# Splitting the next layer's projection weights in sixteen parts inside the layer before it

## The chip, the cores and the metric

One core of one Trainium2 chip runs the whole program. The metric is the device time of one execution in microseconds (us). The kernel before took 4826.84 us (median of three runs, 4824.58 to 4827.53). Lower is better.

## The reference, cut to what matters

Four blocks over 16 sequences of 256 tokens and 128 features, each followed by a layer norm of x plus the block's output. The third is a gated scan, the fourth six layers of local attention with a feed-forward part; the first two (causal attention, a routed feed-forward) are not touched.

```python
    # third block: g, v, d are x times Wg, Wv, Wd plus biases
    x_scan = sigmoid(g) * tanh(v);  a = 0.001 + 0.998 * sigmoid(d)
    h_t = a_t * h_(t-1) + x_scan_t
    # fourth block, per layer i of 6: 16 heads of 64, windows of 32 and the window before
    for i in range(DEPTH):
        x = attn_layer(shift_tokens(x), Wqkv[i], q_scale[i], k_scale[i], Wo[i]) + x
        x = ffn_layer(shift_tokens(x), ln_g[i], ln_b[i], W1[i], b1[i], W2[i], b2[i]) + x
    # attn_layer: qkv = x @ Wqkv (128 x 3072); q and k to unit length, scaled, rotated; softmax in windows; @ Wo
x = _layernorm(x + scan(x)); x = _layernorm(x + six_layers(x))
```

## The kernel before, in words

The stream of tokens stays in SBUF, features on the partitions: `X` is 128 x 16 sequences x 290 columns (34 of padding). Blocks of code follow each other; between two blocks all engines meet at a barrier, and GpSimd clears the block's semaphores one by one (`clear_semaphores`, line 30).

**The gated scan** (`gated_scan`) works a sequence at a time. VectorE scales the normed result into `X0` (line 1758), GpSimd copies it from there into `X` (line 1726). `X0` stays in SBUF through the six layers, since the last norm (`add_and_norm` with tag "o") adds it to the layers' output (line 1518), half a thousand columns at a time, eight times.

**The six layers** (`local_attention_layers`) are 192 tiles of 128 tokens: 6 layers x 16 sequences x 2. Each engine runs its own program of slots; in slot k it works on tile k and on tiles up to seven behind, `tile(n)` being the tile n behind. The functions in `slot` stand in each engine's order. Even slots belong to the first half of a sequence, odd ones to the second; a turn of a loop is one even and one odd slot. TensorE has one flat loop over all sequences (`run_flat`, 92 turns in the middle, so 184 tiles of the 192), in which the layer of tile k is `k >> 5`; the other engines have a loop over layers with four sequences of each layer written out and the rest in an inner loop.

- `product` (TensorE, line 2055) multiplies a tile by a chunk of 512 columns of the layer's weights; there are six chunks, q1, k0, q0, k1, v0, v1. For precision both sides are split in a high part (upper bits) and a low part (the rest), and a product is three matmuls, high x high, high x low, low x high. Each product waits for its chunk's split (line 2052). Within a slot TensorE does q1 and k0, down, centred, q0 and k1, then v1 of the tile before, variance, project, the turns of queries and keys, hidden_up, the turns of attention and probabilities, hidden_gate, scores (128 small matmuls, line 2141), v0, attend (128 small matmuls, line 2174).
- `split_weights` (VectorE, lines 2554 to 2558) makes the two parts of a chunk: a mask by bits into `W_cut`, a copy to `W_high`, a subtraction to `W_low`. Five chunks are split in the first slot of a layer, after the normalised attention and ahead of the tables (line 2540) and the first rotation (line 2572); v1 is split one slot later, since the last tile of the layer before still reads it.
- `load_projections` (SP, line 1974) loads a layer's whole weights (1536 KB) into `W_whole` in one DMA, two slots after the layer's start, for the next layer, and the scales of q and k (line 1975).
- `spread` (SP, lines 1992 to 1996) copies a tile's values into windows, six DMAs in an even slot and eight in an odd one. SP also loads the small weights of each layer one by one as the tile before stops using them (lines 2011 to 2035); while it waits for that, the spreads behind stand.
- GpSimd adds the sine parts (line 2489), multiplies queries and keys by their inverse lengths (line 2499, needs VectorE's line 2593), and splits and shifts the input (lines 2451 to 2476).
- VectorE's slot ends the tile before's key rotation and goes on: squared lengths (2582), gated (2656), denominators (2617, 2619), row maxima (2600, needs the scores), inverse lengths (2589, 2593), centred scores (2609), normalised attention (2627), rotations (2572), and the write of X for the tile seven behind (2664).

## Time and profile before

| what | us |
|---|---|
| median of three runs | 4826.84 |
| the profiled execution | 4830.08 |
| its span, first to last instruction | 4828.3 |
| TensorE busy | 4226.8 |
| VectorE busy | 3910.9 |
| ScalarE busy | 3408.1 |
| GpSimd busy | 2756.9 |

Durations come from the one profiled execution; between its span and its own time lie 1.8 us outside the first and last instruction. In the rows PE is TensorE's matmuls, PEld its weight loads, DVE VectorE, ACT ScalarE, POOL GpSimd and SP SyncE; L12 is line 12. A name with q behind it (PEldq, POOLq, SPq) is the engine's sequencer: register steps, branches, semaphores, the issue of DMAs. Busy time is a union, so that a matmul that overlaps the next counts once.

### The profile page before, as it was taken

Reading aid. Unit: us, or ns where it says so; the run is one execution under the profiler, and the core shown is the slowest. Engines: PE = TensorE matmul, PEld = TensorE weight load, DVE = VectorE, ACT = ScalarE, POOL = GpSimd, SP = SyncE. Lnnn points to the kernel's source line nnn. Section 1 sums busy time; section 2 is a strip of 40 time slices with the busy share of each in tenths; the row PEclk is TensorE's granted clock in tenths of the full one; section 3 lists DMA queues with packets and bytes.
Section 4 is the critical chain, followed back from the end, with each engine's and each line's share of the span. In section 5 each row is a group of like instructions: output and inputs, shape, how many; then the busy total and the mean of one; then the engine's idle time right before and its main releaser. Section 6 shows DMA issues by size and latency. Waiting matters only on the chain. (4 is left out here: it accounts for less than half of the span.)

```text
span 4828.3 us, 192699 instructions
## 1 busy us (share of the span) xinstructions
PE 4226.8 (88%) x74096; PEld 3380.5 (70%) x74097; DVE 3910.9 (81%) x6558; ACT 3408.1 (71%) x5995; POOL 2756.9 (57%) x3213
## 2 busy tenths in 40 slices
PE   7888875697455799999999999989999999999996
PEld 4444432375233688888888888878887888888884
DVE  5777757644446889999999999999999999989995
ACT  4555521254225689888998889879998898889983
POOL 2222213634221767767776777767776777677771
PEclk8999977798777999999999999999999999999997
DMA  3000003252210211111111211121112111121110
GB/s 149 1 0 0 0 0 117 92 197 75 98 57 18 65 38 48 47 55 53 43 47 49 59 48 41 48 59 47 48 42 60 49 46 46 40 69 41 48 45 28
DMA packets 141882, 255.16 MB, mean 53 GB/s; under 512 B 34160, under 2 KB 56944, under 8 KB 137072
## 3 DMA queue, kind: packets, MB, share of 16 engines
q1 hardware_dynamic: 133520, 235.49, 16.5%
q0 software_dynamic: 8192, 17.84, 1.2%
q8 instruction: 53, 0.87, 0.1%
q14 instruction: 117, 0.96, 0.1%
HBM read 70.76 MB, written 44.04 MB: 24 GB/s over the span
## 5 line engine op out<-in xcount | busy, mean ns | idle before, releaser
L2489 POOL TENSOR_TENSOR d_rc<-d_rc,d_rs 128x512 f32<-128x512 f32 x768 | 964.1, 1277 | 479.1 <-DVE d_rs L2572 463.3
L2499 POOL TENSOR_TENSOR d_rc<-d_rc,d_inv 128x1024 f32<-128x1024 f32 x384 | 722.9, 1903 | 123.3 <-DVE d_inv L2593 122.9
L2055 PE MATMUL d_pair<-d_W_high,d_xs_high 128*128 128x512 f32 x1152 | 520.7, 452 | 124.0 <-DVE d_W_low L2558 40.7
L2572 DVE TENSOR_TENSOR d_rc<-d_pair,d_rot 128x512 f32<-128x512 f32 x768 | 527.3, 687 | 97.2 <-ACT d_sq L2304 78.9
L2304 ACT ACTIVATE d_sq<-d_pair 128x512 f32<-128x512 f32 x768 | 435.3, 596 | 144.2 <-PE d_pair L2055 139.0
L2572 DVE TENSOR_TENSOR d_rs<-d_pair,d_rot 128x512 f32<-128x512 f32 x768 | 521.7, 679 | 0.0
L2055 PE MATMUL d_pair<-d_W_high,d_xs_low 128*128 128x512 f32 x1152 | 462.8, 402 | 0.0
L2055 PE MATMUL d_pair<-d_W_low,d_xs_high 128*128 128x512 f32 x1152 | 462.1, 401 | 0.0
L2582 DVE TENSOR_REDUCE d_ss<-d_sq 128x16 f32<-128x1024 f32 x384 | 448.0, 1207 | 0.0
L2202 PE MATMUL d_pair<-d_OT,d_Wo 128*128 128x128 f32 x3072 | 382.8, 279 | 0.0
L2055 PEld LDWEIGHTS d_pair<-d_W_high,d_xs_high 128*128 128x128 f32 x1152 | 220.2, 191 | 212.1 <-issue 153.7
L2099 PE MATMUL d_pair<-d_ident,d_rc 128*128 128x128 f32 x3072 | 367.7, 273 | 1.0 <-ACT d_sq L2304 1.0
L2202 PEld LDWEIGHTS d_pair<-d_OT,d_Wo 128*128 128x128 f32 x3072 | 367.1, 196 | 0.1
L2099 PEld LDWEIGHTS d_pair<-d_ident,d_rc 128*128 128x128 f32 x3072 | 342.8, 142 | 2.1 <-issue 1.7
L2600 DVE TENSOR_REDUCE d_mx<-d_pair 128x16 f32<-128x1024 f32 x192 | 234.5, 1221 | 104.5 <-PE d_pair L2141 104.5
L2141 PEld LDWEIGHTS d_pair<-d_KT,d_QT 64*32 64x32 f32 x24576 | 255.8, 105 | 89.6 <-issue 89.2
L2320 ACT ACTIVATE d_QT<-d_pair 128x1024 f32<-128x1024 f32 x192 | 196.8, 1025 | 158.9 <-PE d_pair L2099 158.9
L2174 PEld LDWEIGHTS d_pair<-d_VW,d_PT 64*32 64x32 f32 x18432 | 253.5, 105 | 76.2 <-issue 76.1
L315 ACT ACTIVATE a_first<-a_bank,a_late_bias,a_later 128x256 bf16<-128x256 f32 x256 | 130.1, 569 | 236.2 <-PE a_bank L163 236.2
L2174 PE MATMUL d_pair<-d_V,d_PT 64*32 64x64 f32 x6144 | 288.1, 227 | 7.1 <-issue 7.1
L2141 PE MATMUL d_pair<-d_KT,d_QT 64*32 64x64 f32 x24576 | 287.9, 225 | 7.3 <-issue 7.3
L2174 PE MATMUL d_pair<-d_VW,d_PT 64*32 64x64 f32 x18432 | 286.6, 227 | 6.5 <-issue 6.5
(370 smaller groups left out, 11236.5 us busy)
## 6 DMA issues: line engine op xcount, KB each, us to landing
d_VW<-d_V SPq DMA_DIRECT2D x768, 128.0 KB
d_VW<-d_V SPq DMA_DIRECT2D x576, 64.0 KB
leaf_rows<-a_zeros SPq DMA_DIRECT2D x12, 1152.0 KB, 14.8
q_xrow<-leaf_rows SPq DMA_DIRECT2D x24, 576.0 KB
leaf_out<-q_yrow SPq DMA_DIRECT2D x24, 512.0 KB
d_W_whole<-Wqkv_dram SPq DMA_DIRECT2D x7, 1536.0 KB, 6.2
f_xrow<-leaf_rows SPq DMA_DIRECT2D x8, 576.0 KB, 3.8
b_table<-q_w_dram SPq DMA_DIRECT2D x4, 1024.0 KB, 9.4
```

The costliest lines, as they stand in the source:

```text
L2055: mm = nc.tensor.matmul(target, x_part[:, t.par, :], w_part[:, c, :], start=n == 0, stop=n == 2)
L2099: mm = nc.tensor.transpose(ps[:, hp // 4, (hp % 4) * 128:(hp % 4) * 128 + 128], source(hp), ident[:])
L2141: mm = nc.tensor.matmul(s_pair[WIN * w:WIN * w + WIN, odd, hp * DH:hp * DH + DH], QT[rows, hp, WIN * w:WIN * w + WIN], KT[rows, hp, at + W ...
L2174: mm = nc.tensor.matmul(o_pair[WIN * w:WIN * w + WIN, odd, hp * DH:hp * DH + DH], PT[rows, hp, WIN * w:WIN * w + WIN], window_values(t, w, ...
L2202: mm = nc.tensor.matmul(proj_bank[:, 0:128], Wo[:, hp, :], OT[:, hp, :], start=hp == 0, stop=hp == HP - 1)
L2304: nc.scalar.activation(sq[:, half, 512 * j:512 * j + 512], ps[:, j, :], ACT.Square).then_inc(s[f"s{qk}{j}_ready"], 1)
L2320: nc.scalar.activation(QT[:].rearrange("p h t -> p (h t)"), flat_pair(qt_pair), ACT.Copy).then_inc(s["qt_ready"], 1)
L2489: nc.gpsimd.tensor_tensor(own[:, :, a, :], own[:, :, a, :], other[:, :, 1 - a, :], ALU.add).then_inc(s[f"add{qk}_ready"], 1)
L2499: nc.gpsimd.tensor_tensor(heads(rc[:, t.par, half, :]), heads(rc[:, t.par, half, :]), inv[:, t.par, half, :].unsqueeze(2).to_broadcast([12 ...
L2572: ins = nc.vector.tensor_tensor(heads(target), heads(ps[:, j, :]), rot[:, t.par, half, cs, :].unsqueeze(1).to_broadcast([128, HP, DH]), AL ...
L2582: nc.vector.tensor_reduce(ss[:, half, :], heads(sq[:, half, :]), AX_X, ALU.add).then_inc(s[f"ss{qk}_ready"], 1)
L2600: nc.vector.tensor_reduce(mx[:], s_pair[:].rearrange("p a (h n) -> p (a h) n", n=DH), AX_X, ALU.max)\
```

## The change

The weights have a second home: `W_high` and `W_low` are twice as long, and a layer's parts stand in the half of its parity. During layer l the weights of layer l + 1 are split in 16 parts of 192 columns, one in each even slot: SP loads the part into `W_stage` (96 KB, two places in turn), VectorE masks it into `W_next`, GpSimd subtracts and copies into the other half. TensorE waits for parts at q1 and v1 only, and reads the weights at a place worked out from the layer's parity. The first layer's weights are loaded whole into `W_first`, which lies in the space of `rc`, and split ahead as before, all six chunks. To make room, the scan's result `X0` is written to DRAM a sequence at a time and read back by the last norm. The part of layer 6 that nobody uses is split as well (96 parts in all, 16 a layer).

```diff
-def add_and_norm(nc, dram, X, Y, tag, leaf=None, out=None, s_out=None):
+def add_and_norm(nc, dram, X, Y, tag, leaf=None, kept=None, out=None, s_out=None):
+        names += [f"y_in{b}" for b in range(NB)]
@@ SP
+            if kept is not None:
+                for b in range(NB):
+                    sp.dma_start(Y[:, BT * b:BT * b + BT], kept[:, BT * b:BT * b + BT]).then_inc(s[f"y_in{b}"], 16)
@@ VectorE, summed(b)
+                if kept is not None:
+                    dve.wait_ge(s[f"y_in{b}"], 16)
@@ gated_scan, SP
+            for k in range(SEQS):
+                sp.wait_ge(s["x_ready"], k + 1)
+                sp.dma_start(kept[:, T * k:T * k + T], X0[:, T * k:T * k + T]).then_inc(s["stored"], 16)
+            sp.wait_ge(s["stored"], 16 * SEQS)
@@ local_attention_layers
-        W_high = sb("d_W_high", [128, W_CHUNKS, 512], F32R)
-        W_low = sb("d_W_low", [128, W_CHUNKS, 512], F32R)
-        W_whole = sb("d_W_whole", [128, W_CHUNKS, 512])
+        W_high = sb("d_W_high", [128, 2 * W_CHUNKS, 512], F32R)
+        W_low = sb("d_W_low", [128, 2 * W_CHUNKS, 512], F32R)
+        W_stage = sb("d_W_stage", [128, 2 * W_PART])
+        W_next = sb("d_W_next", [128, 2 * W_PART])
+        def next_part(w, t):
+            half = (t.l + 1) % 2 if isinstance(t.l, int) else (t.l + 1) & 1
+            return w[:].rearrange("p c n -> p (c n)")[:, bass.ds(half * (W_CHUNKS * 512) + t.b * W_PART, W_PART)]
@@ SP
+            def load_next_part(t):
+                if not t.live or t.par:
+                    return
+                n = t.l * W_PARTS + t.b
+                sp.wait_ge(s["next_split"], n + 1)
+                sp.sem_inc(s["gate_sp"], 1)
+                whole = of_layer("Wqkv", t.l + 1).rearrange("o p c n -> p (o c n)")
+                sp.dma_start(W_stage[:, turn_of(n)], whole[:, bass.ds(t.b * W_PART, W_PART)]).then_inc(s[f"w_in"], 16)
...
                 spread(tile(2))
                 t = tile(2)
                 if t.live and t.first:
-                    sp.wait_ge(s["w_split"], W_CHUNKS * t.l + W_CHUNKS)
-                    sp.sem_inc(s["gate_sp"], 1)
                     sp.wait_ge(s["tables"], 8 * t.l + 8)
                     sp.sem_inc(s["gate_sp"], 1)
-                    load_projections(t.l + 1)
+                    load_scales(t.l + 1)
+                load_next_part(tile(0))
@@ TensorE
+            def weights(w_part, t, c):
+                if t.edge:
+                    return w_part[:, t.l % 2 * W_CHUNKS + c, :]
+                return w_part[:, bass.ds((t.l & 1) * W_CHUNKS + c, 1), :].rearrange("p o n -> p (o n)")
             def product(t, target, what):
                 c = CHUNK_OF[what]
-                if t.first:
-                    pe.wait_ge(s["w_split"], W_CHUNKS * t.l + c + 1)
+                if t.edge:
+                    if t.first:
+                        pe.wait_ge(s["w_split"], c + 1)
+                elif what == "q1":
+                    pe.wait_ge(s["next_split"], t.l * W_PARTS)
+                elif what == "v1":
+                    pe.wait_ge(s["next_split"], t.l * W_PARTS + 2)
                 wait(pe, "xs_split", t)
                 for n, (x_part, w_part) in enumerate(((xs_high, W_high), (xs_high, W_low), (xs_low, W_high))):
-                    mm = nc.tensor.matmul(target, x_part[:, t.par, :], w_part[:, c, :], start=n == 0, stop=n == 2)
+                    mm = nc.tensor.matmul(target, x_part[:, t.par, :], weights(w_part, t, c), start=n == 0, stop=n == 2)
@@ GpSimd, after add_sine_part(tile(2), 0, "q"): next_weights(tile(4)); ahead of all: pool.sem_inc(s["next_split"], 2)
+            def next_weights(t):
+                if not t.live or t.par:
+                    return
+                n = t.l * W_PARTS + t.b
+                pool.wait_ge(s["next_cut"], n + 1)
+                pool.sem_inc(s["gate_pool"], 1)
+                cut = W_next[:, turn_of(n)]
+                nc.gpsimd.tensor_tensor(next_part(W_low, t), W_stage[:, turn_of(n)], cut, ALU.subtract).then_inc(s["next_low"], 1)
+                nc.gpsimd.tensor_copy(next_part(W_high, t), cut).then_inc(s["next_split"], 1)
@@ VectorE; split_weights is left for the first layer alone, mask, subtraction, copy, all six chunks in slot 0
+            def next_cut(t):
+                if not t.live or t.par:
+                    return
+                n = t.l * W_PARTS + t.b
+                dve.wait_ge(s["w_in"], n * 16 + 32)
+                dve.wait_ge(s["next_split"], n + 1)
+                dve.sem_inc(s["gate_dve"], 1)
+                nc.vector.tensor_scalar(W_next[:, turn_of(n)].bitcast(U32), W_stage[:, turn_of(n)].bitcast(U32), 0xFFFFF000, None,
+                                        ALU.bitwise_and).then_inc(s["next_cut"], 1)
...
-                split_weights(tile(1), ("v1",))
                 denominators(tile(3))
+                next_cut(tile(0))
                 row_maxima(tile(2))
                 inverse_lengths(tile(1))
                 centred_scores(tile(2))
                 normalised_attention(tile(3))
-                split_weights(tile(0), ("q1", "k0", "q0", "k1", "v0"))
+                split_weights(tile(0), ("q1", "k0", "q0", "k1", "v0", "v1"))
                 tables(tile(0))
```

## Rows read from the trace of the kernel before

**Rows 1.** The page: busy tenths of TensorE in 40 slices of the span.
```profile
PE   7888875697455799999999999989999999999996
```

**Rows 2.** Windows, one turn (even and odd tile): busy us of PE, PEld, DVE, ACT, POOL; clock; DMA.
```profile
2428.50:2460.30 31.80, 31.35 (x695) 27.81 (x694) 29.92 (x50) 28.74 (x52) 23.74 (x29) 1.00 0.17 45
```

**Rows 3.** Waits in 2240 to 2580, TensorE's only one: us in total, times, longest.
```profile
PE d_pair L2055 <- issue: 4.3, 10, 0.5
```

**Rows 4.** Timeline of VectorE: start, us, instruction; X written for tiles 22, 28 and 32.
```profile
2044.55 0.34 DVE L2664 SCALAR_TENSOR_TENSOR X<-d_pair,d_vecs_a,XM 128x128 f32 x1
...
2151.28 0.34 DVE L2664 SCALAR_TENSOR_TENSOR X<-d_pair,d_vecs_a,XM 128x128 f32<-128x128 f32 x1
...
2219.08 0.34 DVE L2664 SCALAR_TENSOR_TENSOR X<-d_pair,d_vecs_a,XM 128x128 f32<-128x128 f32 x1
```

**Rows 5.** Timelines of VectorE, GpSimd, TensorE at the split; all masks by line (ns min/median/max).
```profile
2090.58 2.08 DVE L2554 TENSOR_SCALAR d_W_cut<-d_W_whole 128x512 uint32<-128x512 uint32 x1
...
2100.01 1.16 DVE L2540 TENSOR_TENSOR d_rot<-d_rot_const,d_qkscale 128x64 f32<-128x64 f32 x8
...
2088.62 3.76 POOL L2499 TENSOR_TENSOR d_rc<-d_rc,d_inv 128x1024 f32<-128x1024 f32 x2 [0.85 <-DVE d_inv L2593]
...
2093.86 0.79 PE L2055 MATMUL d_pair<-d_W_high,d_xs_high 128*128 128x512 f32 x1 [4.83 <-DVE d_W_low L2558]
...
L2554 DVE TENSOR_SCALAR d_W_cut<-d_W_whole x36: 410/427/2079, 1562.1 to 4212.0; 128x512 uint32<-128x512 uint32 x36
```

**Rows 6.** Timelines of SP and VectorE: last DMA of an even spread, steady and late.
```profile
2447.61 0.60 SPq L1996 DMA_DIRECT2D d_VW<-d_V  x1
...
2196.34 0.60 SPq L1996 DMA_DIRECT2D d_VW<-d_V  x1
...
2197.75 1.23 DVE L2600 TENSOR_REDUCE d_mx<-d_pair 128x16 f32<-128x1024 f32 x1 [1.93 <-PE d_pair L2141]
```

**Rows 7.** Timelines of an even slot: VectorE, GpSimd's input split, TensorE's v1 product.
```profile
2451.26 0.25 DVE L2619 RECIPROCAL d_rden<-d_den 128x16 f32<-128x16 f32 x1
2451.86 1.23 DVE L2600 TENSOR_REDUCE d_mx<-d_pair 128x16 f32<-128x1024 f32 x1 [0.35 <-PE d_pair L2141]
...
2456.22 0.69 DVE L2572 TENSOR_TENSOR d_rc<-d_pair,d_rot 128x512 f32<-128x512 f32 x1 [0.46 <-ACT d_sq L2304]
...
2451.61 0.46 POOL L2476 TENSOR_TENSOR d_xs_low<-d_xs,d_xs_high 128x128 fp32r<-128x128 f32 x1
...
2458.32 0.40 PE L2055 MATMUL d_pair<-d_W_high,d_xs_high 128*128 128x512 f32 x1
```

**Rows 8.** Timelines of VectorE and GpSimd at the end of the scan.
```profile
1550.29 0.42 DVE L1758 TENSOR_TENSOR X<-c_xc,c_rstd 128x256 f32<-128x256 f32 x1
...
1550.92 0.40 POOL L1726 COPY X<-X 128x256 f32<-128x256 f32 x1 [4.24 <-DVE X L1758]
```

**Rows 9.** DMA issues: count, KB each, median us to landing.
```profile
out_dram<-X SPq DMA_DIRECT2D x8, 256.0 KB, 2.1
```

**Rows 10.** Register steps by line (ns min/median/max); on TensorE's timeline, an even slot's q1 product.
```profile
L2052 PEldq ALU_OP  x828: 32/32/32, 1697.2 to 4711.3; - x166
...
L1674 PEldq FUSED_REGOPS  x14: 55/62/69, 1456.5 to 1534.9; - x14
...
L963 PEldq ALU_OP  x448: 32/36/41, 936.0 to 1362.5; - x150
...
L963 PEldq FUSED_REGOPS  x256: 55/55/70, 936.1 to 1362.6; - x128
...
L1942 PEldq COMPARE_BRANCH  x92: 76/208/223, 1739.5 to 4713.7; - x92
...
2454.54 0.49 PE L2055 MATMUL d_pair<-d_W_high,d_xs_high 128*128 128x512 f32 x1 [0.41 <-issue]
```

**Rows 11.** GpSimd's first operation in the last norm, and all clears of semaphores.
```profile
4777.74 0.10 POOL L1494 MEMSET o_eps<- 128x1 f32 x1 [19.02 <-POOLq L26]
...
L30 POOLq EVENT_SEMAPHORE_RANGE_CLEAR  x271: 37/44/48, 713.1 to 4827.9; - x136
```

More of the change, by code:

```diff
@@ L1640, in gated_scan @@
         names = """w_in memset_done gates_done gate_ready u_ready a_ready h_ready r_ready mean_done xc_ready
[L1641 removed]
+            xsq_ready var_done std_ready rstd_ready x_ready copied gate stored""".split()
         s = {n: ctx.enter_context(nc.semaphore("c_" + n)) for n in names}
@@ L1782 @@
 W_CHUNKS = len(CHUNK_OF)
+W_PARTS = 16
+W_PART = W_CHUNKS * 512 // W_PARTS
 SPREADS = (6, 8)
@@ L2521, in slot @@
                 add_sine_part(tile(2), 0, "q")
+                next_weights(tile(4))
                 shifted_input(tile(1))
@@ L2544, in split_weights @@
             def split_weights(t, whats):
-                if not (t.live and t.first):
+                if not (t.live and t.first and isinstance(t.l, int)):
                     return
-                dve.wait_ge(s["w_in"], 16 * t.l + 16)
+                dve.wait_ge(s["w_in"], 16)
                 for what in whats:
                     c = CHUNK_OF[what]
-                    wait(dve, f"{what}_done", t, -1)
-                    if c or not isinstance(t.l, int):
-                        dve.wait_ge(s["w_split"], W_CHUNKS * t.l + c)
-                    nc.vector.tensor_scalar(W_cut[:].bitcast(U32), W_whole[:, c, :].bitcast(U32), 0xFFFFF000, None, ALU.bitwise_and)\
+                    if c:
+                        dve.wait_ge(s["w_split"], c)
+                    nc.vector.tensor_scalar(W_cut[:].bitcast(U32), W_first[:, c, :].bitcast(U32), 0xFFFFF000, None, ALU.bitwise_and)\
                         .then_inc(s["w_cut"], 1)
-                    dve.wait_ge(s["w_cut"], W_CHUNKS * t.l + c + 1)
-                    nc.vector.tensor_copy(W_high[:, c, :], W_cut[:]).then_inc(s["w_high"], 1)
-                    nc.vector.tensor_tensor(W_low[:, c, :], W_whole[:, c, :], W_cut[:], ALU.subtract).then_inc(s["w_split"], 1)
+                    dve.wait_ge(s["w_cut"], c + 1)
+                    nc.vector.tensor_tensor(W_low[:, c, :], W_first[:, c, :], W_cut[:], ALU.subtract).then_inc(s["w_low"], 1)
+                    dve.wait_ge(s["w_low"], c + 1)
+                    nc.vector.tensor_copy(W_high[:, c, :], W_cut[:]).then_inc(s["w_split"], 1)
+                dve.wait_ge(s["w_split"], W_CHUNKS)
+            def next_cut(t):
[7 more added lines that the diff above has]
+                                        ALU.bitwise_and).then_inc(s["next_cut"], 1)
             def rotated(t, half, qk, j):
@@ L2759, in build @@
         fast_feedforward_block(nc, dram, X, rows_dram, out_dram, scattered, gathered, arrived, bias_dram)
-        X0 = ctx.enter_context(nc.sbuf_tensor("X0", [128, SEQS * T], F32))
-        gated_scan(nc, dram, X, X0)
+        kept = nc.dram_tensor("scan_out", (128, SEQS * T), F32).ap()
+        with ExitStack() as inner:
+            X0 = inner.enter_context(nc.sbuf_tensor("X0", [128, SEQS * T], F32))
+            gated_scan(nc, dram, X, X0, kept)
         with ExitStack() as inner:
@@ L2764, in build @@
             local_attention_layers(nc, dram, X, XM)
-        add_and_norm(nc, dram, X, X0, "o", out=out, s_out=s_out)
+        X0 = ctx.enter_context(nc.sbuf_tensor("X0_again", [128, SEQS * T], F32))
+        add_and_norm(nc, dram, X, X0, "o", kept=kept, out=out, s_out=s_out)
 def kernel(**inputs):
```

19 lines of the change are left out of this document (11 added, 8 removed).

## The prediction

> **What bounds the kernel now.** I read the page first: span 4828.3 us, and from slice 15 on TensorE is at 9 tenths in nearly every slice [rows 1], so two thirds of the span is the six layers. Next came the windows of one even and one odd tile (two tiles are one turn of the loop): 31.80 us with TensorE busy 31.35, VectorE 29.92, ScalarE 28.74, GpSimd 23.74, at clock 1.00 [rows 2]. The waits of a steady stretch say who yields: VectorE and ScalarE wait for TensorE, GpSimd for VectorE, and TensorE waits for nobody; its idle time is "issue", 10 times 0.43 us in 10.7 turns [rows 3]. So in a layer TensorE sets the pace of 15.88 us a tile, and VectorE has 1.9 us to spare in a turn (31.80 - 29.92). Last, the timeline of VectorE's X writes (one a tile): from tile 22's to tile 28's 106.73 us pass where six steady tiles take 95.3, and from there to tile 32's 67.80 for 63.5 [rows 4]. A change of layer loses 11.4 us around the weight split and, four tiles later, 4.3 us. My readings of the other four changes are 12.9, 13.0, 11.4, 12.7 and 4.3, 4.1, 4.1, 5.2, in all 61.4 and 22.0 us.
>
> The first loss is the split: VectorE spends 2090.58 to 2100.01 on five chunks (9.43 us; the first mask takes 2.08 us, the median one 427 ns), and TensorE stands 4.83 us before the first product of the layer [rows 5]. The second loss is another matter: SP is held by the small weights' waits, the last DMA of the spread starts at 2196.34, 1.4 us before VectorE's row maxima of that slot, where in steady state it starts 4.25 us before them [rows 6, 7].
>
> **Part 1, the split leaves the boundary.** The 15 instructions of the block go, the three of v1 one tile later too. What stays is the eight table products, 1.16 us [rows 5]. They delay the first rotation, and VectorE's idle before it (0.46) takes a part; the v1 product needs that rotation and has 0.8 us of margin (2458.32 against 2456.22 and two of 0.69, which overlap a little: 2457.5) [rows 7]. I leave 1.0 us a boundary, 5 in all: gain 61.4 - 5 = **56**. Bounds: 50 (2.3 stays each) to 61.
>
> **Part 2, VectorE's mask in every even tile.** 96 masks of 192 columns. 512 columns take 427 ns [rows 5], so 192 take between 160 (by columns alone) and 427, and I take 260 for a fixed part. It stands after the denominators' reciprocal, which ends at 2451.51, and before the row maxima, which wait for TensorE until 2451.86 [rows 7]. 0.35 us of idle cover 0.26; the register steps of its waits lie under the instruction before. If the cover goes, 0.46 us of idle before the rotation catch it. Cost 0. Above: GpSimd. The first mask of the layer ended at 2092.66, 0.28 us after GpSimd's pair of products (2088.62 + 3.76 = 2092.38) [rows 5]: such a mask does not run beside a GpSimd instruction. At 2451.51 GpSimd is at its input splits of 0.46 us, and its 1.9 us products cannot be there, since they wait for inverse lengths that VectorE makes only later in the slot [rows 7]. So at most 0.26 + 0.46 = 0.72, against 0.81 of idle in the slot: 0 again. The Trainium skill has this as a rule (SBUF — State Buffer, "SBUF: two separate sides"): the pair of ports is an exclusive lock, whoever starts first keeps it for the whole instruction. By that rule the sum is the same unless the longer GpSimd products are met, which rival C prices.
>
> **Part 3, GpSimd.** Subtraction and copy of 192 columns each: two inputs of 128 columns take 0.46 and of 1024 columns 1.88 (half of 3.76), the copy of 256 takes 0.40, so 0.56 + 0.35 and some 0.2 around them, 1.1 us a turn [rows 5, 7, 8]. GpSimd has 8 us a turn to spare [rows 2]. It delays the next slot's input split by up to 1.1; the even slot's is ready at 2451.61 + 0.46 = 2452.07 and its first product starts at 2454.54 [rows 7, 10], so there are some 2.5 us of cover and nobody waits. Cost 0; below 0 nothing, as work is only added; above, 0.3 us in each of 96 turns, if its products of the next slot start that much later and somebody waits, = 29.
>
> **Part 4, SP and the parts' arrival.** One more DMA behind the even spread's six, whose last issue ends at 2448.21 [rows 6]. A wait that is long satisfied, register steps and issue put the DMA at about 2448.6. It carries 96 KB; 256 KB land 2.1 us after issue [rows 9], so it lands at about 2450.7, 0.8 us before the mask asks. Cost 0 in steady state. In the slot with the late spread it does not fit: issue after 2196.94, landing near 2199.4, where VectorE's row maxima began at 2197.75 [rows 6]. VectorE comes 1.6 to 2 us late, 0.46 at least is caught by idle before the rotation, and TensorE's margin of 0.8 takes most of the rest: 0.5 a boundary, **2.5** in all (0 to 10). The next spread is 11 us away, and the burst of 1536 KB at each change of layer goes, which nobody waited for.
>
> **Part 5, TensorE's sequencer.** This is the price that decides. In the loop the weights now stand at a place worked out from the layer's parity: for each product two addresses, and of the six waits on the split two remain. The waits cost 828 small register steps in 92 turns, 9 a turn [rows 10]. Of address work there are two kinds of rows: three products sharing one simple address cost 14 steps in 14 slots, one each; an address with shift and mask (the table products) costs (448 + 256)/256 = 2.75 steps, and those are hidden under long matmuls, the matmuls that follow them show next to no idle. Inside a product (0.7 us of matmuls) I cost them at nothing, the matmuls cover them. But right behind the 128 small matmuls of "attend" nothing covers: the loop's branch adds 208 ns and two register steps there, and the even q1 product that follows shows 0.41 us idle, where the odd one shows none (one idle spot a turn) [rows 3, 10]. One step there costs about 0.12 us. How many are new? The wait is swapped one for one; an address is at least one step, at most 2.75, and some may be shared with the slot before. I take 1.25, 0.15 us a tile, 184 loop tiles: **+28**. Bounds: -9 (a saved wait at v0, behind the scores, and shared addresses) and 0.4 x 184 = +74.
>
> **Part 6, the ends.** The scan's block now ends with the last store: ready at 1550.71, plus 2.1 us for such a store, against 1551.32 for the end of GpSimd's copy [rows 8, 9]: **+1.5**. The last norm starts when the first 256 KB are back, 2.1 us and some 0.2 of issue after 4777.74, and the chain of the norm follows from its first sum [rows 9, 11]: **+2.3** (2 to 5). 21 more semaphores are cleared, 44 ns busy each [rows 11] and 0.067 with what lies between: **+1.4**. The first layer splits six chunks ahead instead of five, in three steps that no longer overlap, and saves the late v1: 0 (-1 to +3).
>
> **Sum.** -56 + 0 + 0 + 2.5 + 28 + 1.5 + 2.3 + 1.4 = -20.3. The profiled execution took 4830.1 (span 4828.3 and 1.8 around it), so 4809.8; the median of the three runs shown is 3.2 lower, 4826.84, so **4806**.
>
> **Rivals.** A, the sequencer hides it all: then -48.3, 4778.5 (with the saved wait 4770). For it: the table products' steps were hidden. Against: they stood behind long matmuls. B, the other side: the addresses are worked out afresh at q1. Without this part the change is worth 48.3 us, so it ends slower once 0.26 us a tile, some two steps, are exposed there; at 0.4 us it is 4826.8 - 48.3 + 74 = 4852. For it: 2.75 steps is the row nearest in form, with two addresses a product. Against: repeated expressions are shared in the scan's row. C, VectorE's mask meets a long GpSimd product or a part lands late in every turn: 1.9 + 0.26 - 0.81 = 1.35 us x 96 = 130, 4936; a part 1 us late gives (1.26 - 0.81) x 96 = 43, 4849. Against: the order of the slot. D, the change doesn't remove the loss at the boundary, since GpSimd's last parts or the tables hold TensorE: with half the gain left 4834. By the order of the slots the last part is split more than half a slot before the v1 product that needs it, so this has little for it.
>
> **How the numbers follow.** My forecast (4790 to 4822) has 0.50, A (below 4790) 0.17, B 0.20, C 0.09, D 0.04. A measurement of this kernel tells 0.2% (9.7 us) from no change. Below 4817.2 lie A and most of the forecast: 0.66. Within 4817.2 to 4836.5 lie the forecast's upper edge, half of B and D: 0.19. Above: 0.15. The range leaves out the deep end of A, and of B and C what is above 4838: 4776 to 4838.
>
> **What would show it.** Right: X writes 15.9 us apart through the change of layer but for 1 us, the 4.83 us idle gone, the clock 1.00 all through; the mask near 0.26 to 0.7 us in VectorE's idle before the maxima; two idle spots of TensorE at q1, near 0.55 in even and 0.15 in odd slots, a turn of 32.1 us instead of 31.8. Wrong: a turn still at 31.8 (A), or above 32.3 (B), masks of 1 to 2 us or waits on the stage's DMA in steady turns (C), a gap before the first product of a layer (D).

## The result, and the profile after

The changed kernel takes 4840.28 us (median of 20 runs, 4829.81 to 4850.72) where the kernel before takes 4824.19 on the same chip (20 runs): ratio 1.0034, 95% interval 1.0027 to 1.0041, 16 us slower. I had forecast 4806, 20 us faster; the time lies above the end of my range. The two profiled executions (4830.1 and 4833.4) stand only 3.3 us apart. The memset of c_eps, the start of the scan, ahead of which only eight more semaphores are cleared, comes 13 us earlier in the one of after (1431.6 against 1444.7), so I compare stages: the scan takes 112.1 us (108.4 before), the layers 3234.0 (3224.7), the last norm 54.0 (50.5), together 16.4 us more.

Of the page, the row that answers [rows 1], and the windows of one turn (columns as in [rows 2]):

```profile
span 4831.6 us, 196107 instructions
...
PE   7888875697445899999999999999999999999996
```
```profile
2418.29:2434.62 16.33, 15.82 (x347) 14.06 (x348) 15.23 (x25) 14.38 (x26) 12.88 (x17) 1.00 0.18 48
2434.62:2450.47 15.85, 15.47 (x346) 13.66 (x346) 15.16 (x26) 14.29 (x26) 11.55 (x15) 1.00 0.18 48
sum 32.18, PE 31.29 PEld 27.73 DVE 30.38 ACT 28.67 POOL 24.43; mean PE 15.65 PEld 13.86 DVE 15.19 ACT 14.34 POOL 12.22
```

The turn is 32.18 us, not 31.80. TensorE is busy as long as before (31.29 against 31.35); what grew is its idle time. Next come the largest wait of TensorE in the same steady stretch as [rows 3] (besides it there is one of 0.8 us for GpSimd's split of the input), and TensorE's timeline at an even and an odd q1 product:

```profile
PE d_pair L2097 <- issue: 9.1, 21, 0.7
```
```profile
2450.75 0.49 PE L2097 MATMUL d_pair<-d_W_high,d_xs_high 128*128 x1 [0.66 <-issue]
...
2466.63 0.49 PE L2097 MATMUL d_pair<-d_W_high,d_xs_high 128*128 x1 [0.23 <-issue]
```

Idle "issue" went from 4.3 to 9.1 us, and it now stands ahead of each q1, not of every second. The line of the products' matmuls, which had no register steps before, has the ones below. The 828 of [rows 10] belonged to the waits on the split; in their place stand 184, one a tile.

```profile
L2097 PEldq ALU_OP  x1380: 32/32/36, 1694.0 to 4715.4; - x198
...
L2097 PEldq FUSED_REGOPS  x1104: 55/60/69, 1694.1 to 4715.3; - x184
```

Two of them stand between the branch and the even q1 product at 2450.75 (the same line, from 2450.5 to 2450.75), where before there was none of this line:

```profile
L2097 PEldq ALU_OP  x1: 36/36/36, 2450.5 to 2450.5; - x1
L2097 PEldq FUSED_REGOPS  x1: 60/60/60, 2450.6 to 2450.6; - x1
```

The change of layer is read from X's writes for tiles 22, 28 and 32, as in [rows 4]:

```profile
2041.42 0.34 DVE L2732 SCALAR_TENSOR_TENSOR X<-d_pair,d_vecs_a,XM 128x128 f32 x1
...
2141.84 0.34 DVE L2732 SCALAR_TENSOR_TENSOR X<-d_pair,d_vecs_a,XM 128x128 f32<-128x128 f32 x1
...
2212.10 0.34 DVE L2732 SCALAR_TENSOR_TENSOR X<-d_pair,d_vecs_a,XM 128x128 f32<-128x128 f32 x1
```

Six tiles take 100.42 us (before 106.73), the four behind them 70.26 (before 67.80). So the split did leave the boundary, but less came of it than I had booked, and the second loss grew. At the start of the layer VectorE and GpSimd show this (compare [rows 5]):

```profile
2084.03 0.26 DVE L2625 TENSOR_SCALAR d_W_next<-d_W_stage 128x192 uint32<-128x192 uint32 x1 [0.46 <-issue]
...
2088.03 2.84 DVE L2596 TENSOR_TENSOR d_rot<-d_rot_const,d_qkscale 128x64 f32<-128x64 f32 x8
2091.22 0.69 DVE L2640 TENSOR_TENSOR d_rc<-d_pair,d_rot 128x512 f32<-128x512 f32 x1 [0.36 <-DVE d_rot L2596]
```
```profile
2086.07 3.77 POOL L2541 TENSOR_TENSOR d_rc<-d_rc,d_inv 128x1024 f32<-128x1024 f32 x2 [0.98 <-DVE d_inv L2661]
```
```profile
PE d_pair L2097 <- DVE d_rs L2640: 2.1, 1, 2.1
```

The eight table products take 2.84 us in place of 1.16: the first of them lasts until GpSimd's second long product ends (2086.07 + 3.77 = 2089.84). TensorE stands 2.1 us here and 3.0 to 3.2 us at the other four changes, for the rotation behind them. All runs are laid side by side here, from their traces: the layers' stage (memset of d_eps to that of o_eps), the steady turn, and the means over the five changes of layer of the six tiles and of the four behind them, all in us.

| run | ratio to before, 95% | layers | turn | six | four |
|---|---|---|---|---|---|
| before | 1 | 3224.7 | 31.77 | 107.6 | 67.9 |
| after (the change) | 1.0034 [1.0027, 1.0041] | 3234.0 | 32.17 | 102.2 | 70.2 |
| before_address | 0.9999 [0.9990, 1.0008] | 3222.4 | 31.77 | 107.8 | 68.2 |
| before_parity | 1.0088 [1.0071, 1.0104] | 3261.0 | 32.22 | 109.7 | 68.5 |
| before_kept | 1.0007 [0.9998, 1.0016] | 3219.8 | 31.76 | 108.0 | 68.4 |
| static_address | 0.9951 [0.9936, 0.9966] | 3189.7 | 31.72 | 100.7 | 69.2 |
| after_no_parts | 0.9932 [0.9916, 0.9948] | 3176.1 | 31.71 | 98.8 | 68.5 |
| after_tables_first | 1.0001 [0.9991, 1.0011] | 3214.4 | 32.17 | 98.6 | 70.1 |
| after_load_first | 1.0045 [1.0028, 1.0061] | 3235.1 | 32.17 | 102.4 | 70.0 |
| after_part3_early | 1.0027 [1.0016, 1.0037] | 3231.2 | 32.17 | 102.3 | 69.4 |
| after_by_layers | 1.0000 [0.9991, 1.0010] | 3217.5 | 31.73 | 104.7 | 69.9 |
| after_by_layers_tables_first | 0.9971 [0.9961, 0.9982] | 3202.6 | 31.74 | 102.0 | 69.9 |
| after_v0_last | 0.9895 [0.9880, 0.9909] | 3158.1 | 31.09 | 100.7 | 69.9 |
| before_v0_last | 0.9853 [0.9840, 0.9866] | 3152.6 | 30.75 | 106.4 | 66.9 |
| before_v0_last_again | 0.9855 [0.9842, 0.9867] | 3158.2 | 30.74 | 106.4 | 67.2 |
| after_by_layers_tables_first_v0_last | 0.9915 [0.9902, 0.9929] | 3175.3 | 31.00 | 103.3 | 69.7 |
| after_tables_part3_v0 | 0.9841 [0.9828, 0.9853] | 3141.0 | 31.09 | 96.8 | 69.3 |
| after_tables_part3_v0_again | 0.9856 [0.9841, 0.9871] | 3138.3 | 31.09 | 96.8 | 69.1 |
| after_tables_part3_v0_no_mask | 0.9827 [0.9813, 0.9840] | 3132.5 | 31.09 | 96.3 | 68.2 |
| after_tables_part3_v0_split_on_gpsimd | 0.9979 [0.9969, 0.9988] | 3209.1 | 32.09 | 98.3 | 68.8 |

The runs lie on several chips. On two of them the kernel before takes 5031 us in place of 4822 to 4824; the 200 us lie ahead of the layers (d_eps at 1755 us in before_address, 1553 in before), the layers' stage and the turn are the same. Ratios are to the kernel before on the same chip.

### The profile page after: what moved, and what is told of

Same layout as the page of the kernel before. It is cut to its first block and busy times, and to the rows that moved or that the text cites. A ratio compares the mean times of both kernels' runs of the same rounds, so it can differ in the third digit from the quotient of the medians.

```text
span 4831.6 us, 196107 instructions
## 1 busy us (share of the span) xinstructions
PE 4205.7 (87%) x74096; PEld 3366.4 (70%) x74097; DVE 3914.5 (81%) x6564; ACT 3409.5 (71%) x5995; POOL 2827.3 (59%) x3405
## 5 line engine op out<-in xcount | busy, mean ns | idle before, releaser
L2097 PE MATMUL d_pair<-d_W_high,d_xs_high 128*128 (+1 forms) x1152 | 518.3, 450 | 146.9 <-issue 75.4
L2097 PE MATMUL d_pair<-d_W_high,d_xs_low 128*128 (+1 forms) x1152 | 461.0, 400 | 0.0
L2097 PE MATMUL d_pair<-d_W_low,d_xs_high 128*128 (+1 forms) x1152 | 459.7, 399 | 0.0
```

The costliest lines, as they stand in the source:

```text
L2097: mm = nc.tensor.matmul(target, x_part[:, t.par, :], weights(w_part, t, c), start=n == 0, stop=n == 2)
```

## The experiments

### Is the longer turn TensorE's address work?

static_address fixes the weights' place in TensorE's code:

```diff
-                return w_part[:, bass.ds((t.l & 1) * W_CHUNKS + c, 1), :].rearrange("p o n -> p (o n)")
+                return w_part[:, c, :]
```

> This is the changed kernel, but TensorE always reads the first home of the weights, at a fixed address, and GpSimd writes all parts into the second (so layers 2 to 6 compute with the first layer's weights; the work and its shapes are the same). Theory S, two register steps exposed ahead of every q1 product cost 0.20 us a tile: the turn falls from 32.18 us back to 31.8, TensorE's idle time at q1 from 0.64 and 0.25 us (even, odd) to 0.42 and 0, and the time by 37 us, from 4840 to 4803 (ratio to the kernel before 0.9957). Rival V, the longer turn comes from the work added in each turn (VectorE's mask, GpSimd's two instructions, the DMA), not from TensorE's addresses: the turn stays at 32.2 and the time at 4840 (ratio 1.003).

before_address and before_parity put the address work into the kernel before, which has neither mask nor parts in its turn:

```diff
+                return w_part[:, bass.ds((t.l & 8) + c, 1), :].rearrange("p o n -> p (o n)")      (before_address)
+                return w_part[:, c, bass.ds((t.l & 1) * 8, 512)]                                   (before_parity)
```

> This is the kernel before, with one thing alone of the change: in the loop TensorE works out the weights' address of each product from the layer's number (a bit of it that is always zero, so the same weights are read). Theory S: the turn rises from 31.77 to 32.1 or 32.2 us, idle at q1 from 0.41 and 0 to some 0.64 and 0.25, and the time by about 37 us, to 4861 (ratio 1.0077). Rival V: a turn of 31.8 us and 4824 (ratio 1.000).

> This is the kernel before, with TensorE's address worked out in the loop from the layer's parity, as the change has it, but only 8 columns apart (each chunk has 520 columns in place of 512; odd layers read their weights 8 columns further, so they compute with shifted weights; the work is the same). before_address did not do this: its trace has the same register steps as before, the bit was known to be zero, so that run was a second copy of the kernel before (0.9999). Theory S: each product gains a step or two, two of them stand exposed ahead of q1; the turn rises from 31.77 to 32.1 to 32.2 us, idle at q1 from 0.41 and 0 to 0.64 and 0.25 us, ratio 1.0075. Rival V: turn 31.8, ratio 1.000.

Measured: without the address work the turn falls to 31.72 us, with it alone the kernel before rises to 32.22. The waits of static_address (340 us of steady stretch) and of before_parity (as long), and before_parity's steps:

```profile
PE d_pair L2096 <- issue: 4.1, 10, 0.4
```
```profile
PE d_pair L2060 <- issue: 8.7, 21, 0.7
```
```profile
L2060 PEldq ALU_OP  x1380: 32/32/36, 1694.0 to 4747.3; - x198
...
L2060 PEldq FUSED_REGOPS  x1104: 46/46/60, 1694.1 to 4747.2; - x184
```

The counts of steps on the product's line are those of the change, and so are the idle spots: 21 again, one a tile. Theory S holds, from both sides. The address work is worth 0.40 us a turn between the kernels before and after (32.17 - 31.77), 0.45 in before_parity and 0.45 in static_address: 0.20 to 0.23 us a tile. before_address changed nothing, since the bit was known to be zero and no step was made (its sequencer's counts are those of before): it is a second copy of the kernel before, whose 0.9999 shows what a null looks like.

### What do the parts cost?

after_no_parts is static_address without the load, the mask and GpSimd's two instructions.

```diff
-                nc.vector.tensor_scalar(W_next[:, turn_of(n)].bitcast(U32), W_stage[:, turn_of(n)].bitcast(U32), 0xFFFFF000, None,
-                                        ALU.bitwise_and).then_inc(s["next_cut"], 1)
...
-                nc.gpsimd.tensor_tensor(next_part(W_low, t), W_stage[:, turn_of(n)], cut, ALU.subtract).then_inc(s["next_low"], 1)
-                nc.gpsimd.tensor_copy(next_part(W_high, t), cut).then_inc(s["next_split"], 1)
+                pool.sem_inc(s["next_split"], 1)
```

> This is the fixed-address kernel of static_address with the work on the parts left out: no DMA, no mask, no subtraction and copy (layers 2 to 6 compute with the first layer's weights). Against static_address (0.9951 with a turn of 31.72 us) it tells what that work costs. As predicted, it costs nothing in a steady turn (31.7 us in both) and some 1.5 us at a boundary: ratio 0.993 to 0.994. Rival P, the work costs up to 0.3 us a turn, hidden so far under the gain of a saved wait: a turn of 31.4 us, ratio 0.989.

The turns are 31.71 and 31.72: in a steady turn the parts are free. At a change of layer they cost 1.9 us of the six tiles and 0.7 of the four, 13 us in all (layers' stage 3189.7 against 3176.1); I had expected 1.5 a boundary. The prediction had put them at nothing there, but for the late part.

### What is left at the start of a layer?

```diff
                 next_cut(tile(0))
+                tables(tile(0))
                 row_maxima(tile(2))
...
-                tables(tile(0))
                 rotated(tile(0), 0, "q", 1)
```

> This is the changed kernel, but the eight table products stand ahead of the row maxima, where GpSimd runs short copies, and not ahead of the first rotation, where they wait for the port of its 1.9 us product. Theory T (the port wait of the tables, 1.9 us, is what is left of the boundary's loss): six tiles around the start of a layer take 100.5 in place of 102.3 us, TensorE's idle of 2.1 to 3.0 us in front of v1 is gone, 2 us at each of 5 boundaries, 10 us in all (ratio about 1.001 in place of 1.0034). Rival U (the loss comes from elsewhere, for instance from the start and end of the loops and the late parts): six tiles stay at 102 us, ratio 1.003.

VectorE's timeline of after_tables_first at the second layer change of its trace, then TensorE's longest wait in 2600 to 2625 in after and in after_tables_first:

```profile
2610.57 1.36 DVE L2596 TENSOR_TENSOR d_rot<-d_rot_const,d_qkscale 128x64 f32<-128x64 f32 x8
```
```profile
PE d_pair L2097 <- DVE d_rs L2640: 3.0, 1, 3.0
```
```profile
PE d_pair L2307 <- DVE d_sc L2677: 0.8, 1, 0.8
```

The eight products take 1.36 us, TensorE's 3.0 us wait for the rotation is gone (0.8 remain, ahead of the down product). Six tiles take 98.6 us in place of 102.2, 3.5 us less, where I had expected 1.8; the time falls by 0.33% (16 us), the layers' stage by 19.6. Theory T holds, but the wait for GpSimd is only part of the gain: it made the first product 1.7 us longer (2.84 - 1.16), and the move also takes the products' own 1.2 us from ahead of the rotation; the last 0.6 us of the 3.5 were not traced. This one move of eight small instructions is worth as much as the change lost.

### The second loss: the late part, or something behind it?

```diff
+                load_next_part(tile(0))
                 spread(tile(2))
...
-                load_next_part(tile(0))
```

> This is the changed kernel with the load of the next part ahead of the spread in SP's order, not behind it (and SP waits for the part before it to be in, so that the two are told apart). Theory L: the waits on the stage's DMA (6.7 us in three waits in the first layer change) go; the four tiles behind the layer's start take 68.5 in place of 70.2 us (before: 67.7), 1.5 us at each of 5 boundaries, 7 us in all; nothing in the steady turn. Rival M: the four tiles stay at 70, the loss there comes from the late spread as before and from the mask. Above: if the extra DMA delays the spread in every turn, the turn rises above 32.2 us.

Theory L fell: four tiles take 70.0 us, with 70.2 in the change. VectorE's waits on the stage over the first layer change went, and TensorE's wait stayed. In this order: VectorE in after, VectorE in after_load_first, TensorE at that slot in after, in after_load_first, and in before:

```profile
DVE d_W_next L2625 <- DMA d_W_stage<-Wqkv_dram: 6.7, 3, 4.0
```
```profile
DVE d_W_next L2627 <- DMA d_W_stage<-Wqkv_dram: 0.4, 1, 0.4
```
```profile
PE d_pair L2097 <- ACT d_G L2450: 1.6, 1, 1.6
```
```profile
PE d_pair L2099 <- ACT d_G L2452: 1.6, 1, 1.6
```
```profile
PE d_pair L2055 <- ACT d_G L2408: 0.4, 1, 0.4
```

TensorE waits for ScalarE's gelu, and ScalarE for its bias:

```profile
ACT d_G L2450 <- DMA d_vecs_g<-vecs_g_dram: 2.4, 1, 2.4
```

(1.5 us before). SP's timeline in after and in before tells why; the late even spread ends with the first line of each:

```profile
2188.23 0.49 SPq L2028 DMA_DIRECT2D d_VW<-d_V  x1
2189.08 0.36 SPq L2004 DMA_DIRECT2D d_W_stage<-Wqkv_dram  x1
2189.78 0.34 SPq L2060 DMA_DIRECT2D d_vecs_g<-vecs_g_dram  x1
```
```profile
2196.34 0.60 SPq L1996 DMA_DIRECT2D d_VW<-d_V  x1
2197.30 0.34 SPq L2029 DMA_DIRECT2D d_vecs_g<-vecs_g_dram  x1
```

Counted from tile 28's X write, vecs_g is issued at 47.9 us in place of 46.0 (47.6 to 47.9 at the five changes), behind the part's load; ahead of the spread the load delays it just as much (47.7). So after_part3_early takes that one load away from it:

```diff
+                load_fourth_part(tile(-1))      (in the odd slot ahead, behind its spread, for the fourth part of a layer alone)
```

> This is the changed kernel with the fourth part of each layer loaded one slot earlier, behind the odd spread and ahead of the waits for the small weights, so that no part's DMA stands between the late spread and the DMA of vecs_g. Theory G (the loss is vecs_g, issued 1.7 us later, for which ScalarE's gelu and then TensorE wait): vecs_g is issued 46.0 to 46.3 us after tile 28's X write in place of 47.9, TensorE's idle of 1.2 to 1.6 us at that q1 falls to 0.6, and the four tiles take 69 in place of 70.1 us: 5 us in all, ratio 1.0024. Rival N, the mask itself or its waits delay VectorE there: 70 us and 1.0034 as before.

vecs_g is issued at 46.9 to 47.5, TensorE's wait is 0.8 to 1.0 us in place of 1.2 to 1.6, the four tiles take 69.4 in place of 70.2:

```profile
PE d_pair L2110 <- ACT d_G L2463: 1.0, 1, 1.0
```

Theory G holds in direction and half in size. With vecs_g at 46.0 TensorE's 0.4 us are those of any even q1 [rows 10]; at 46.9 to 47.5 it stands 0.8 to 1.0, at 47.6 to 47.9 (the change and after_load_first) 1.2 to 1.8. The ratio moved by 0.0007, within both intervals; the four tiles are what the run shows.

The lines above tell where the 1.9 us come from. Behind the first line of each, from the last spread to vecs_g 1.55 us pass in place of 0.96: 0.6 us are the load's. The spread itself stands 1.3 us later (46.39 against 45.06), and most of that goes with VectorE's mask: after_part3_early, which has it, still issues vecs_g about 1.2 us late, while after_no_parts and after_tables_part3_v0_split_on_gpsimd, which do not have it, issue it at 45.9 to 46.2. Between after_tables_part3_v0 and the same kernel without the mask it is 1.2 us as well (47.5 against 46.3, means of five). The longer turn alone (before_parity) gives 46.3. So rival N holds in part, by a path that no run takes apart. A delay of this kind needs no change, either: at the fifth change of the kernel before vecs_g is issued at 47.1, and the four tiles take 68.8 us in place of 67.6 to 67.8.

### The ends

before_kept is the kernel before with the store and the read-back of the scan's result.

> This is the kernel before with the scan's result stored to DRAM and read back for the last norm, and nothing else of the change. By the sum of the prediction's part 6 it costs 1.5 + 2.3 and some 0.4 for the added semaphores, 4 us (ratio 1.0009); from the two profiles of before and after I read 3.7 us more in the scan and 3.4 more at the end, 7 us (ratio 1.0015).

3.5 us, with an interval from -1 to 8: both sums fit. In the trace of after the read-back is issued at 4777.60 and the first sum starts 2.96 us later, where it started at once before (4777.78):

```profile
4777.60 3.67 SPq L1433 DMA_DIRECT2D X_again<-scan_out  x8
...
4780.56 0.69 DVE L1524 TENSOR_TENSOR o_r<-X,X_again 128x512 f32<-128x512 f32 x1 [9.21 <-DMA X_again<-scan_out]
```

The last stage is 3.4 us longer. The scan took 109.3 to 112.4 us in the 15 traces with the store and 107.3 to 109.7 in the five without it; 3.1 us lie between the means. Why this is twice the 1.5 of the prediction was not looked for.

### Can the steps be taken off the path?

after_by_layers writes TensorE's loop once for each parity, so that only v1 of odd tiles still has an address to work out:

```diff
+            layer(0, UNROLLED, SEQS)
+            with eng.Fori(0, (LAYERS - 2) // 2) as two:
+                layer(1, two * (2 * SEQS) + SEQS, two * (2 * SEQS) + 2 * SEQS)
+                layer(0, two * (2 * SEQS) + 2 * SEQS, two * (2 * SEQS) + 3 * SEQS)
+            layer(1, (LAYERS - 1) * SEQS, LAYERS * SEQS)
```

> This is the changed kernel with the right result and without the address steps at q1: TensorE's loop over the tiles is written once for each layer's parity (first layer, a loop over two pairs, last layer), so that the home of the weights is fixed in the code for all products but v1 of odd tiles. Theory S: the turn is 31.7 to 31.8 us in place of 32.17 and the time 37 us less, but for what entering five more loops costs (some 0.5 to 4 us each): 4805 to 4820 on the first chip, ratio 0.996 to 1.000. Rival: code that is fetched anew at each loop costs it all: 1.003.

> Both repairs together: fixed homes in TensorE's code and the table products ahead of the row maxima. If the two effects are independent, 0.9951 (fixed address) less 0.0033 (tables first) = 0.992, and up to 0.996 if entering the loops costs a few us each. Rival: the two losses hide each other, 0.995 or above.

The turn is 31.73 as foreseen, but the changes of layer, where TensorE now enters another loop, are dearer: six tiles take 104.7 us where static_address took 100.7, and the four 0.7 more, 23 us in all. In TensorE's waits over the first layer change (85 us) idle "issue" has spread to new places; over those ten tiles it sums to 4.3 to 8.8 us, with 2.2 to 2.6 in static_address. That this is the fetching of new code was not shown.

```profile
PE d_pair L2124 <- issue: 2.7, 5, 1.0
...
PE d_pair L2243 <- issue: 1.0, 2, 0.7
```

The time is that of before (1.0000), and 0.9971 with the tables moved, so the two repairs add up.

The other way is to cover the spot. v0 behind attend lays its three matmuls over the branch and over q1's steps:

```diff
-                values(tile(0), 0)
                 attend(tile(2))
+                values(tile(0), 0)
```

> This is the changed kernel with TensorE's order changed in one place: the v0 product comes behind attend instead of ahead of it, so that its three matmuls of 512 columns (0.7 us) lie over the branch and the steps of the next q1. Theory S: the idle time at q1 (0.64 + 0.25 us a turn) goes nearly whole; up to 0.89 us x 92 turns = 80 us, a turn of 31.3 us and 4760 us (ratio 0.987). Rival W: v0's result comes 1.9 us later, so ScalarE's copy, the spread or the q0 product that waits for the bank come late in turn, and the idle moves there: a turn of 31.9 to 32.2 or more, 4815 to 4840.

> This is the kernel before with the v0 product behind attend instead of ahead of it. Theory S: the 0.41 us of idle at the even q1 go, 31.4 us a turn, 38 us less: 4786 (ratio 0.992); the same order in the changed kernel is then some 25 us faster than this one, as the address steps cost nothing any more and only the change of layer is left. Rival W: the idle moves to the bank of v0 or to VectorE, and both stay within 10 us of where they were.

> Both repairs, and the v0 product behind attend, which took 1.5% from the kernel before (0.9853) and left the changed kernel 0.34 us a turn slower than it. Theory S (that 0.34 us are the address steps of v0 and q1, now in one stretch that the sequencer bounds): the turn falls to the 30.75 us of before_v0_last, and with a boundary that is 7 to 9 us shorter at each of five changes of layer the time is 35 to 45 us below before_v0_last: ratio 0.977. Rival: VectorE (its mask, 30.2 us of work a turn) is now the bound, the turn stays at 31.0, ratio 0.982 to 0.984.

The order is worth about twice the time that I expected: the kernel before gains 1.5% (turn 30.75 in place of 31.77, against 31.4 expected), more than its 0.4 us of recorded idle. In the window of one turn of before_v0_last_again TensorE is busy without a gap, and busy 0.6 us less than in [rows 2]:

```profile
2375.39:2406.13 30.74, 30.74 (x693) 27.85 (x693) 29.52 (x49) 28.52 (x51) 23.68 (x29) 1.00 0.17 47
```

So lost time also lay inside rows that count as busy. The starts of the matmuls tell which. In the kernel before, v0's first matmul and the first of attend lie 0.89 us apart, while three matmuls in a run of nine take 0.73; from attend's first to q1's 1.53 us pass in an odd slot and 1.89 in an even one, while from attend's first to v0's in before_v0_last it is 1.40 in both. That is 0.32 and 0.62 us a turn, nearly all of the 1.02. That it is the sequencer which holds the long matmuls back between the small ones is likely, not shown. The changed kernels gained as much but stayed 0.25 to 0.34 us a turn behind, so the last run's 30.75 was not reached. Is it VectorE's mask? With the fourth part early and the tables moved, once as it is, once with the whole split on GpSimd, once without the mask:

```diff
-                next_cut(tile(0))
...
-                cut = W_next[:, turn_of(n)]
+                cut = W_stage[:, turn_of(n)]      (without the mask)
```

> The changed kernel with the tables ahead of the row maxima, the fourth part early and v0 behind attend; addresses worked out in the loop as in the change. after_v0_last stood at 0.9895; less 0.0033 for the tables and 0.001 for the part: 0.985, a turn of 31.09 us. If the gains of the boundary don't add to those of the turn: 0.988.

> As after_tables_part3_v0, but VectorE has no part in the split: GpSimd cuts the high part itself by a product with 4097 and two subtractions of 192 columns (some 0.55 us each), then the subtraction and the copy as before, 2.8 us in a turn in place of 1.0. Theory V2 (with TensorE's idle gone, the 0.26 us mask and its waits on VectorE are on the path): the turn falls from 31.09 to 30.8 us and the time by 25 us, ratio 0.980. Theory S2 (the address steps of v0 and q1 bind): the turn stays at 31.0 to 31.1, ratio 0.985. Rival: GpSimd becomes late and the turn rises.

> As after_tables_part3_v0, but VectorE's mask is left out: GpSimd subtracts the part from itself and copies it whole, so the products of layers 2 to 6 see an unsplit high part and a low part of zeros; the number and the size of the other instructions, the DMA and TensorE's address steps are the same. Theory V2 (the mask is on VectorE's path): the turn falls from 31.09 to 30.85 us, 22 us in all, ratio 0.9795. Rival S2 (address steps, GpSimd or the DMA hold the rest): the turn stays at 31.05 to 31.1, ratio 0.984.

> The same kernel as before_v0_last, beside the two above on one chip: ratio 0.985 again, a turn of 30.75 us. It is the kernel that a repaired change has to beat.

> The fastest kernel so far, again: ratio 0.984, turn 31.09 us.

It is not: without the mask the turn is 31.09 as with it. At the changes of layer the mask does cost something: without it the six tiles take 96.3 us in place of 96.8, the four 68.2 in place of 69.1 to 69.3, and the layers' stage 5.8 to 8.5 us less. The whole split on GpSimd told nothing of this, since GpSimd came late itself; TensorE's waits in 2240 to 2500 have one row:

```profile
PE d_pair L2112 <- POOL d_xs_low L2535: 5.8, 8, 0.7
```

The rest is seen where an address is still worked out. TensorE's timeline of after_by_layers_tables_first_v0_last at v1 of an odd tile, from the last matmul of k1 on, and the same place in before_v0_last:

```profile
2601.86 0.40 PE L2124 MATMUL d_pair<-d_W_high,d_xs_low 128*128 128x512 f32 x1
2602.27 0.50 PE L2124 MATMUL d_pair<-d_W_high,d_xs_high 128*128 x1
2602.61 0.40 PE L2124 MATMUL d_pair<-d_W_low,d_xs_high 128*128 x1
2602.84 0.39 PE L2124 MATMUL d_pair<-d_W_high,d_xs_low 128*128 x1
```
```profile
2584.84 0.40 PE L2055 MATMUL d_pair<-d_W_high,d_xs_low 128*128 128x512 f32 x1
2585.08 0.40 PE L2055 MATMUL d_pair<-d_W_high,d_xs_high 128*128 128x512 f32 x1
2585.32 0.39 PE L2055 MATMUL d_pair<-d_W_low,d_xs_high 128*128 128x512 f32 x1
2585.55 0.40 PE L2055 MATMUL d_pair<-d_W_high,d_xs_low 128*128 128x512 f32 x1
```

Matmuls start 0.24 us apart where the address is fixed, 0.41 and 0.34 apart at this v1: 0.27 us too late in all, once a turn, and the turn is 0.25 longer. Yet no idle stands in the row.

The kernels that keep one loop lose theirs behind the branch, where v0's 0.73 us do not cover the branch and the address steps together. TensorE's timeline of after_tables_part3_v0, the last matmul of v0 and the first two of q1:

```profile
2254.65 0.39 PE L2110 MATMUL d_pair<-d_W_high,d_xs_low 128*128 x1
2255.16 0.49 PE L2110 MATMUL d_pair<-d_W_high,d_xs_high 128*128 x1
2255.49 0.40 PE L2110 MATMUL d_pair<-d_W_low,d_xs_high 128*128 x1
```

v0, q1 and k0 take 2.53 us there in most turns, in the other slot 2.20, and in before_v0_last 2.20 to 2.23 in both: 0.33 us once a turn, which is the whole distance (31.09 against 30.75). A kernel with that v1 fixed too was not run, so all this is read from the traces, not shown by a run.

The fastest kernel that has the change is after_tables_part3_v0, 0.9841 and 0.9856 in its two runs. It beats the kernel before by about 1.5% and the change by more, but nearly all of that is the order of v0. Against before_v0_last its layers' stage is 12 to 20 us shorter, and some 6 us go back in the scan and the last norm. On one chip the medians are 4746.4 and 4752.4 (4741.4 to 4749.4 and 4747.4 to 4766.6): in favour of the change, not told apart.

## Why the prediction was wrong

Point by point, predicted against measured, in us over the run:

- **Part 1, wrong in size: -56 predicted, about -33 measured.** "I leave 1.0 us a boundary" is the step that failed. What is left is 102.17 - 3 x 32.17 = 5.7 us a boundary. Moving the tables takes 3.5 of them away (after_tables_first), leaving the parts out 1.9 (after_no_parts against static_address). I took 1.16 us for the tables from a row in which they ran free, and called the 2.08 us of the first mask in [rows 5] a price of the mask. It was the price of whoever stands there while GpSimd runs its pair of long products: with the split gone the first table product inherits it (2.84 in place of 1.16, at each of the five changes). This wait is 1.7 of the 3.5 us, and the products' own 1.2 are my 1.0. The parts' 1.9 us I had put at nothing, because I looked for their cost in the steady turn. So of the 4.7 us that I was short 1.7 are the wait, 1.9 the parts, and about 1 was not traced. The Trainium skill (SBUF — State Buffer, "Who interferes with whom") says that a VectorE instruction with two SBUF inputs contends with a GpSimd instruction that reads SBUF; the tables have two, and the trace agrees. I had weighed that lock for the new mask and not for the instruction that moved into its place.
- **Part 2, right in the turn, not at the change of layer.** The masks take 0.26 us where their address is fixed and 0.39 in the loop, and cost nothing in a turn (31.71 and 31.72 without and with the parts). Their rows by line:

```profile
L2625 DVE TENSOR_SCALAR d_W_next<-d_W_stage x96: 259/389/827, 1553.1 to 4683.3; - x72, 128x192 uint32<-128x192 uint32 x24
```

  The 0.46 us of "issue" ahead of a mask I had not foreseen; the turn does not feel it. At a change of layer the mask costs about 1.5 us of the ten tiles (after_tables_part3_v0_no_mask), which is part of what Parts 1 and 4 missed.
- **Part 3, right** in steady turns by the same pair of runs.
- **Part 4, right in the place, wrong in who waits: +2.5 predicted, +7 measured**: the four tiles grew by 2.24 us at each of five changes, of which 0.80 is the longer turn's. I priced VectorE's wait for the part, which after_load_first removed for nothing. What TensorE felt was vecs_g, the gelu bias, queued behind the spread and the new DMA on SP and issued 1.6 to 1.9 us later; only 0.6 us of that are the new DMA's.
- **Part 5, mechanism right, the term too small: +28 predicted, +37 measured** (0.405 us a turn x 92). Two steps are exposed ahead of q1, not 1.25. In all a tile has 9.5 steps more than before, although the waits' steps go (828 and 276 of the longer kind, which I had not counted); what the turn shows is the price of those two. With idle of 0.66 and 0.23 us where I had forecast 0.55 and 0.15, the turn is 32.17, just above the 32.1 that I had named.
- **Part 6: +5.2 predicted, about +6 measured**: 3.4 for the last stage against 2.3 and its share of the 1.4 for semaphores, some 3.1 for the scan against 1.5. The first layer starts 2.2 us later (192.2 us from the memset of d_eps to the fourth X write, 190.0 before), within my -1 to +3.

In the two profiles the terms sum to -33 + 7 + 37 + 2 = +13 for the layers, where the stage grew by 9.3. The last seven tiles, 3.9 us shorter in the profile of after (66.0 against 69.9), fill the gap, and that is chance: in before_kept and before_address, with the layers of the kernel before, they take 63.1 and 66.5. With 7.1 for the scan and the last norm it is 16.4, against 16.1 between the medians. By terms the error is 23 for the boundary, 9 for the steps, 4.5 for SP's queue. So my rival B (the address work) was the right one to fear, but by my own threshold, 0.26 us a tile, it would not have decided at 0.20; it decided because the gain it was set against was 23 us smaller.

## What to carry to other kernels

When a block of work leaves a place, ask what will stand there next and which of the removed prices it inherits: a long first instruction in a group can be a wait for somebody, not a size. Look for the cost of spread-out work at the irregular places too, not only in the steady turn. A DMA added to a queue is paid by what is issued behind it, not only by who waits for its data. Address work that depends on a loop was free here inside a run of long matmuls (q0, k1 and v1 take 2.19 us with and without it in the kernels with one loop; the v1 above is the exception) and cost 0.1 us a step behind many small ones or a branch; one long product moved onto that spot took 72 to 76 us off the kernel before.

## What the runs showed of the hardware that I had not expected

- TensorE's added register steps are busy 32 to 69 ns each, and the two ahead of q1 delay it by 0.20 to 0.23 us: about 0.1 us a step from start to start.
- Rows of matmuls can be without idle though the matmuls start late: reordering took 1.02 us off a turn whose recorded idle was about 0.4, and at a v1 with address steps ahead of it matmuls of 0.40 us started 0.41 apart in place of 0.24.
- A product of 128x64 (eight of them take 1.16 us when free) lasted 1.9 us, until GpSimd's product ended, at each of the five changes of layer.
- In the kernel whose code has a loop for each parity a change of layer takes about 4.6 us longer (104.7 + 69.9 against 100.7 + 69.2); 2.1 to 6.6 us more idle "issue" is recorded there, spread over several products.
